# A language-model layer on one core: which engine copies the first probabilities, adds the word and position rows, and writes the first keys

## The reference

```python
h = gamma * norm(word_emb[ids] + pos_emb + type_emb[types]) + beta
a = norm(h)
k, q, v = heads(a @ Wk), heads(a @ Wq), heads(a @ Wv)          # 16 heads of 16
k, q = norm(k) * kln_w + kln_b, norm(q) * qln_w + qln_b        # over the 16 of a head
attn = softmax(where(causal, q @ k.T / 4, -inf))
h = h + (attn @ v) @ Wo + bo
x = norm(h)
scores = softmax(x @ gate_w.T); sel = top_k(scores + expert_bias, 2)
h = h + sum over the two chosen experts e of  score_e-weighted  (silu(xe @ w1[e]) * (xe @ w3[e])) @ w2[e]
```

## Time and profile before

| what | value |
|---|---|
| median of 3 runs | 545.32 us (545.27 to 545.44) |
| time of the profiled execution | 545.62 us |
| its span (first to last instruction) | 543.8 us |
| busy: PE, DVE, ACT, POOL | 501.2, 291.9, 250.7, 286.2 us |
| shares of the last-ending chain: PE, DVE, POOL, ACT | 79%, 5%, 5%, 4% |
| stretch 100 to 120 us, busy: PE, DVE, ACT, POOL | 18.52, 17.63, 17.50, 14.93 us of 20 |
| stretch 180 to 200 us, busy: PE, DVE, ACT, POOL | 17.16, 18.00, 16.35, 14.71 us of 20 |

### The profile page before, as it was taken

The page is one execution under the profiler, slowest core; times in us unless marked ns, Lnnn a source line. Parts: engine busy times, 40 slices in busy tenths (PEclk is TensorE's granted clock), DMA queues, the critical chain, the costliest instruction groups (busy, mean ns, idle before and its releaser), DMA issues.

```text
span 543.8 us, 13452 instructions
## 1 busy us (share of the span) xinstructions
PE 501.2 (92%) x4470; PEld 428.7 (79%) x4471; DVE 291.9 (54%) x759; ACT 250.7 (46%) x575; POOL 286.2 (53%) x532
## 2 busy tenths in 40 slices
PE   5877989998999888999999999999999999999991
PEld 2345666777776665499999999999999999999980
DVE  2778888889989887733333333333333333333330
ACT  1166788978997883243223322332233323332320
POOL 4678787677764675214543454345434454344432
PEclk9999999999999999999999999999999999999996
DMA  5007721101028672302212221122112221222221
GB/s 174 10 22 243 231 85 31 58 29 29 29 80 278 212 251 84 90 22 41 29 30 39 39 39 22 37 39 39 23 36 39 39 28 31 39 38 30 30 39 19
DMA packets 29962, 36.75 MB, mean 68 GB/s; under 512 B 8272, under 2 KB 23504, under 8 KB 29936
## 3 DMA queue, kind: packets, MB, share of 16 engines
q0 software_dynamic: 8352, 12.76, 13.8%
q1 hardware_dynamic: 20768, 22.61, 13.1%
q10 hardware_dynamic: 816, 1.06, 0.6%
HBM read 26.81 MB, written 9.50 MB: 67 GB/s over the span
## 4 chain that ended last, share of the span: by engine, by line
PE 79%; DVE 5%; POOL 5%; ACT 4%; issue 3%; DMA 2%; POOLq 0%; DVEq 0%; ACTq 0%
PE PS L1445 35%; PE PS L1456 18%; PE PS L1172 10%; PE PS L1296 5%; PE PS L1254 2%; PE PS L1395 2%; PE PS L1271 2%; DMA x_pair<-word_dram,idx 1%; PE PS L1180 1%; ACT work L628 1%; PE PS L1310 1%; PE PS L1243 1%; DVE nmax L879 1%; DMA out_dram<-x_pair,dst_c 1%; POOL arena L477 1%
## 5 line engine op out<-in xcount | busy, mean ns | idle before, releaser
L1445 PEld LDWEIGHTS PS<-work,arena 128*128 128x128 f32 x1716 | 197.6, 192 | 2.3 <-ACT work L744 0.4
L1445 PE MATMUL PS<-work,arena 128*128 128x128 f32 x1716 | 198.0, 275 | 0.0
L750 ACT ACTIVATE work<-PS 128x768 f32<-128x768 f32 x39 | 31.6, 810 | 197.2 <-PE PS L1445 197.2
L1456 PE MATMUL PS<-w_sb,work 128*128 x468 | 107.6, 379 | 0.7 <-DVE x_pair L1147 0.7
L1139 DVE TENSOR_TENSOR work<-work,PS 128x640 f32<-128x640 f32 x39 | 32.0, 821 | 138.0 <-ACT work L750 138.0
L1456 PEld LDWEIGHTS PS<-w_sb,work 128*128 128x128 f32 x468 | 85.9, 190 | 11.2 <-issue 1.1
L572 POOL DMA_INDIRECT out_dram<-x_pair,dst_c x39 | 79.2, 2030 | 21.9 <-POOL dst_c L571 20.5
L571 POOL COPY dst_c<-dest_i 128x1 int32 (+1 forms) x39 | 7.1, 183 | 138.7 <-DVE x_pair L1147 136.5
L628 ACT ACTIVATE work<-PS,nmax 128x128 f32<-128x128 f32 x256 | 72.0, 401 | 3.7 <-DVE nmax L879 3.7
L740 ACT ACTIVATE arena<-w_sb 128x1408 f32 x40 | 55.1, 1379 | 12.0 <-DVE er_i L1115 9.0
L1172 PE MATMUL PS<-ident,work 128*128 128x128 f32 x336 | 54.8, 276 | 1.8 <-ACT work L628 1.8
(11 more groups left out here) (172 smaller groups left out, 618.8 us busy)
## 6 DMA issues: line engine op xcount, KB each, us to landing
w_sb<-w_dram SPq DMA_DIRECT2D x16, 640.0 KB, 5.6
w_sb<-w_dram SPq DMA_DIRECT2D x8, 704.0 KB, 4.5
x_rows<-x SPq DMA_DIRECT2D x16, 128.0 KB, 2.3
out_dram<-arena SPq DMA_DIRECT2D x16, 128.0 KB, 2.4
w_sb<-w_dram SPq DMA_DIRECT2D x16, 64.0 KB, 6.2
w_sb<-w_qkv_dram ACTq DMA_DIRECT2D x1, 768.0 KB, 8.2
work<-x_rows,src_c POOLq DMA_INDIRECT x41, 2.8
out_dram<-x_pair,dst_c POOLq DMA_INDIRECT x39
```

What stands on the lines that cost most here:

```text
L1445: last = n.matmul(up_ps[p][:, i, c, :], ws[p][:, k, at:at + P], xT_sb[p][:, k, :], start=(k == 0), stop=(k == DK - 1))
L1456: last = n.matmul(PS[:, 7, 0:D], hT_sb[p][:, i, :], w2_sb[:, bass.ds(e, 1), i, :], start=(i == 0), stop=(i == FK - 1))
```

## The change

Five edits, all in the attention part:

1. From step 2 on, DVE makes the copy of group 0 of the turned probabilities (`transposed_first`, after `keys_out` in its queue). ACT keeps it in steps 0 and 1. The copy has its own semaphore, `probsT0_ready`; PE's `outputs` and `mask_banks` wait for both.
2. The addition of word rows and `x_base` moves from DVE to POOL (`x_sum`) for sequences 5 to 15, that is in steps 1 to 11. It stands after POOL's square roots at the start of the step and before the next `gather`.
3. From step 2 on, DVE's `sum_rows` (now only mean and variance) stands behind the normalization of sequence t-2 (`x2`), not ahead of it.
4. For sequences 0, 1 and 2 ACT writes the keys itself, ahead of the queries, and waits for `qk_ps` (PE's transposes) instead of `k_ready`; DVE's `keys_out` for these goes.
5. In step 0 ACT's `queries_out(1)` stands ahead of `transposed(2)`.

```diff
+        KEYS_BY_ACT = 3
...
+                def x_sum(u, q, n):
+                    pool.wait_ge(x_base_ready, u + 1)
+                    pool.wait_ge(gathered[q], 16 * (n + 1))
+                    g.tensor_tensor(x_in[q], x_in[q], x_base, ALU.add).then_inc(x_summed, 1)
...
+                    if valid(t + 4) and not at_step(t, 0):
+                        x_sum(t + 4, p, half(4))
                     if valid(t + 5):
                         gather(t + 5, 1 - p, link)
...
-                    a.activation(probsT[:, r * 512:(r + 1) * 512], PS[...], ACT.Copy).then_inc(probsT_ready, 1)
+                    a.activation(probsT[:, r * 512:(r + 1) * 512], PS[...],
+                                 ACT.Copy).then_inc(probsT0_ready if r == 0 else probsT_ready, 1)
...
                 def queries_out(u):
-                    act.wait_ge(k_ready, u + 1)
+                    if isinstance(u, int) and u < KEYS_BY_ACT:
+                        act.wait_ge(qk_ps, u + 1)
+                    else:
+                        act.wait_ge(k_ready, u + 1)
...
+                    if isinstance(u, int) and u < KEYS_BY_ACT:
+                        a.activation(kT.rearrange("p b s -> p (b s)"), PS[:, T_BANK, D:2 * D], ACT.Identity,
+                                     scale=cols_sb[:, 4:5], bias=cols_sb[:, 5:6]).then_inc(k_ready, 1)
...
                     transposed(0)
                     transposed(1)
+                    queries_out(1)
                     transposed(2)
-                    queries_out(1)
...
-                if valid(t):
+                if at_step(t, 1):
                     transposed(0)
...
+                def transposed_first():
+                    dve.wait_ge(probsT_ps, RG * t + 1)
+                    wait(dve, pv_done, t)
+                    v.tensor_copy(probsT[:, 0:512], PS[:, 0, :]).then_inc(probsT0_ready, 1)
...
+                    if isinstance(u, int) and u < EARLY:
+                        dve.wait_ge(x_base_ready, u + 1)
+                        dve.wait_ge(gathered[q], 16 * (n + 1))
+                        v.tensor_tensor(x, x, x_base, ALU.add).then_inc(x_summed, 1)
...
-                    keys_out(0)
...
+                if valid(t) and not at_step(t, 0) and not at_step(t, 1):
+                    transposed_first()
...
-                    keys_out(1)
...
-                    keys_out(2)
...
-                if valid(t + 4) and valid(t):
+                if valid(t + 4) and valid(t) and (at_step(t, 0) or at_step(t, 1)):
                     sum_rows(t + 4, p, half(4))
...
                     normalize(x2[p][:, :], row(u), 2).then_inc(x2_ready, 1)
+                if valid(t + 4) and valid(t) and not at_step(t, 0) and not at_step(t, 1):
+                    sum_rows(t + 4, p, half(4))
...
-                    pe.wait_ge(probsT_ready, RG * u + RG)
+                    pe.wait_ge(probsT0_ready, u + 1)
+                    pe.wait_ge(probsT_ready, (RG - 1) * u + RG - 1)
```

More of the change, by code:

```diff
@@ L224, in build_tower @@
         s_done, max_done, exp_done = sem("s_done"), sem("max_done"), sem("exp_done")
-        probsT_ps, probsT_ready, pv_done, o_ready = (
-            sem("probsT_ps"), sem("probsT_ready"), sem("pv_done"), sem("o_ready"))
+        probsT_ps, probsT_ready, probsT0_ready, pv_done, o_ready = (
+            sem("probsT_ps"), sem("probsT_ready"), sem("probsT0_ready"), sem("pv_done"), sem("o_ready"))
         o_raw_ready, o_back, oT_ps, oT_ready, wo_done = (
@@ L634, in transposed @@
                     wait(act, pv_done, t)
-                    a.activation(probsT[:, r * 512:(r + 1) * 512], PS[:, T_BANK if r == RG - 1 else r, :], ACT.Copy).then_inc(probsT_ready, 1)
+                    a.activation(probsT[:, r * 512:(r + 1) * 512], PS[:, T_BANK if r == RG - 1 else r, :],
+                                 ACT.Copy).then_inc(probsT0_ready if r == 0 else probsT_ready, 1)
                 def x2_out(u):
@@ L920, in sum_rows @@
                                                ALU.add).then_inc(x_base_ready, 1)
-                    dve.wait_ge(x_base_ready, u + 1)
-                    dve.wait_ge(gathered[q], 16 * (n + 1))
-                    v.tensor_tensor(x, x, x_base, ALU.add).then_inc(x_summed, 1)
+                    if isinstance(u, int) and u < EARLY:
+                        dve.wait_ge(x_base_ready, u + 1)
+                        dve.wait_ge(gathered[q], 16 * (n + 1))
+                        v.tensor_tensor(x, x, x_base, ALU.add).then_inc(x_summed, 1)
                     dve.wait_ge(x_summed, u + 1)
@@ L1235, in mask_banks @@
                     pe.wait_ge(exp_done, RG * u)
-                    pe.wait_ge(probsT_ready, RG * u - 1)
+                    pe.wait_ge(probsT0_ready, u)
+                    pe.wait_ge(probsT_ready, (RG - 1) * u - 1)
                     n.matmul(PS[:, RG - 2, 0:E], identb[:, :], mask[:, 0:E], start=True, stop=True)
@@ L1346, in step @@
                     if not edge or t > 0:
-                        pe.wait_ge(probsT_ready, RG * t)
+                        pe.wait_ge(probsT_ready, (RG - 1) * t)
                     transposes(qkn, 2 * DK, T_BANK).then_inc(qk_ps, 1)
```

## The result

The changed kernel takes 547.24 us (median of 6 runs, 546.82 to 549.05), the kernel before, timed in turn with it, 545.47 us (6 runs, 545.27 to 546.01). The ratio is 1.0038, with a 95% interval of 1.0027 to 1.0049: slower by 1.8 us. Forecast were 547.1 us and a range of 544.3 to 548.6.

The account below looks back on a forecast made before the run. No engine had much to give; PE's chain ran nearly unbroken in the loop, DVE, POOL and ACT bounding start and steps 12 to 15. Terms -2.1 +1.2 +0.7 +0.7 +0.6 +0.55 +0.1 = +1.75 us: median 547.1, range 544.3 to 548.6.

Parts of the forecast that it names:

- Start, -2.1: Before step 0: with early keys on idle ACT, PE's first scores start at about 29.1 instead of 31.24, -2.1 us.
- Step 1, +1.2: Step 1: POOL's sum stands behind its square root L437, giving back 1.2 of the 2.1 us gained.
- Steps 2 and 3, +0.7: Steps 2 and 3: POOL's sum and constant tables delay DVE's division and PE's transposes, +0.7 us.
- Steps 4 to 10, +0.7: Loop: longer wait order before PE's weight load, 0.16 us a pass, 0.64 in all, and a little for step 4.
- The ring: From step 2: POOL's sum, DVE's division and POOL's next square roots form a closed cycle of 10.93 us against 10.88.
- PE absorbs waits and ring: Rival, chance 0.23: the loop's wait list costs nothing, POOL's cycle stays just under the step; 546.0 us.
- Step 12, +0.6: Step 12: the copy moves DVE's division, making PE's transposes wait, +0.6 us.
- Step 14, +0.55: Step 14: DVE has no gap up to the maxima of step 15, so the copy costs +0.55 us.
- The copy, 0.60: DVE from step 2 on: group 0's copy takes 0.60 us, with ends 0.42 and 0.68.
- ACT's wait in front of L678: Sign, loop: if ACT's idle time before its copy does not grow, the prediction is wrong about the bound.
- ACT was the bound: Rival, chance 0.17: loop waits for ACT's exponentials are real, so fewer copies free -2.9 us; 544.2 us.
- The sum and `x2` block each other: Rival, chance 0.12: lock or register waits add 0.3 us to POOL's cycle from step 3 on; 549.1 us.

Follow-up runs that it names:

- e1: The kernel before with only the early keys on ACT and the changed order in step 0: 544.97 us, ratio 0.9994.
- e11: The e5 kernel with three more 128x512 matmuls on PE in step 0, behind the seven already there: 544.18 us, ratio 0.9969.
- e13: The e11 kernel with a dead 128x1 copy on DVE in step 1, behind two long-met waits: 543.49 us, ratio 0.9962.
- e2: The kernel before with only the sum moved to POOL and DVE's statistics behind x2: 547.74 us, ratio 1.0036.
- e4: The kernel before with only the copies' count split into two semaphores, all work where it was: 545.63 us, ratio 0.9992.
- e8: The changed kernel with one more small unread copy on POOL ahead of its sum in each loop step: 547.86 us, ratio 1.0036.
- e3: The kernel before with only the group 0 copy on DVE from step 2 on, with the two semaphores: 548.51 us, ratio 1.0047.
- e7: The changed kernel with ACT making the group 0 copy again from step 12 on: 545.95 us, ratio 1.0004.
- e10: The changed kernel with DVE's statistics of the sum ahead of x2 again in every step: 552.6 us, ratio 1.0127.
- e6: The changed kernel with DVE still adding the rows of sequence 5 in step 1: 546.21 us, ratio 1.0014.
- e5: The e1 kernel with six 128x512 matmuls in PE's idle time of step 1: 543.94 us, ratio 0.9968.
- e12: The e11 kernel with ACT's queries of sequence 1 behind its third copy in step 0 again: 544.12 us, ratio 0.997.

## Why the prediction was right

The direction, the start, step 1, step 3 and the price of the copy in step 12 came out as forecast. That the sum came out to 0.02 us (+1.75 forecast, +1.77 measured) is luck. Read from the table, with -2.1 for start and step 0, the terms were put too high by 1.29 us: 0.58 in steps 4 to 11, 0.25 in step 14, 0.17 in steps 2 and 3, 0.11 in step 12, 0.1 for the wait lists, 0.08 in step 1. Missing were 1.28 us: 0.56 in step 13 and 0.72 in and behind step 15.

- **Start, -2.1: right.** The first scores stand at 28.39 to 28.91 us in the ten kernels with early keys, at 30.75 to 31.24 in the four without: -2.3 between the means (28.67, 30.99), of which step 0 gives back 0.2 to 0.3 (the whole change, e1, e11, e13): about -2.1 is left.
- **Step 1, +1.2: right**, +1.12 in the change and +1.06 in e2. PE's transposes stand at 50.49 instead of 51.1, because this execution began early.
- **Steps 2 and 3, +0.7: right**, +0.53 and +0.57.
- **Steps 4 to 10, +0.7: the step that failed.** +0.16 in step 4, nothing behind it. "From the end of ACT's copy to PE's weight load it is ... 0.23": the longer wait came as forecast and cost nothing; in e4 a hidden gap of about 0.1 us in PE's rows took it. The ring was priced at 10.93 us against a step of 10.88. The step is 10.85 in the mean (79.10 to 144.22 for six steps), and e8 puts the ring 0.03 under it. So its size was off by about 0.1 us, and with it the sign. Of the rival "PE absorbs waits and ring" that half is true.
- **Step 12, +0.6: right**, +0.49. Step 13, which I expected free, has +0.56: 0.46 of it goes with the idle time in DVE's queue, which belongs to none of the edits and is gone in e13.
- **Step 14, +0.55: too much there, too little behind it.** +0.30, and +0.72 more in and behind step 15, where e3 has +0.87 and e7 +0.13. I had given step 15 room in DVE's queue; the copy stands there too, in front of the last routing work. With the copy left on ACT there (e7) this goes.
- **The copy, 0.60; the wait lists, +0.1.** 0.60 is what the next instruction stands behind it (103.12 to 103.72). The lists cost 0 (e4).

Of its own signs, two did not come. In step 12 PE waits 0.21 us for `o_n`, not 0.5. And ACT's wait in front of L678 has not grown: 11.1 us in eight steps before and after, 1.59 for 1.62 us in the rows above. The prediction called that a sign of being wrong about the bound; it was a bad sign. The time of the copy went elsewhere in ACT's step, 0.2 to 0.3 us of it into the wait for the keys, and PE's loop stayed as long as it was (-0.04).

Of the rivals, the runs speak against *ACT was the bound*: with a copy less, PE waits 2.0 us for the exponentials instead of 2.1. No run took work from ACT in the loop without giving it to DVE, so that is as far as it goes. *The sum and `x2` block each other* is right in its mechanism and wrong in its price. I had judged `x2` unblocked by a row of 0.41 us from step 3; in the first steps of a pass the same trace has 0.60 or 0.61, each ending 0.08 or 0.09 us behind POOL's `gather` (116.71 and 116.62 in the rows of e10). In the changed kernel it takes 0.66 to 0.81 us in the six steps in which it starts 0.06 to 0.22 us behind the sum, 0.48 or 0.49 where it starts 0.39 us behind, and 0.38 to 0.44 in seven of ten steps of e10. The Trainium skill, "SBUF — State Buffer" (section "SBUF: two separate sides"), calls the port pair of VectorE and GpSimd an exclusive lock held for the whole instruction; the trace agrees: `x2` ends 0.15 or 0.16 us behind the sum in all ten steps (104.42 and 104.26 in the rows above), whenever it starts. But it costs next to nothing, because the statistics behind it wait for the same sum and start at 104.34, 0.08 us behind it (0.03 or 0.04 where no `x2` is in the way). Put ahead of `x2`, they cost 0.45 us a step (e10): edit 3 is what made the sum bearable.

## What to carry to other kernels

Two engines' work moved in opposite directions can be free together and dear apart: undo each part by itself before you judge one. An idle engine is slack only if what it waits for does not come from itself; follow the wait round once, and load it by a known bit to measure the rest. A gain at the start of a pipeline stays only where the narrow engine (here POOL) gets it too, and where nothing is added in front of it: the early keys alone have a median 0.9 us lower here, within the noise, 1.6 to 1.8 with PE kept busy and 2.2 in the best version (e13, 543.49 us), and the other two moves spent all of it.

## What the runs showed of the hardware

- After an idle time of 1.26 to 1.45 us in step 1 PE's clock fell to 0.50 in the traces of e1, e4, e6, e7 and e8, and stayed at 1.00 in those of before, after, e2, e3 and e10, which have that idle time as well. It went with 0.75 and 0.86 us more in e4 and e1. With six matmuls in the gap of step 1 (e5, e11, e12, e13) it fell in none of four traces.
- In step 0 it fell in e5 and e7 at 35 us, with 1.5 us more there, half of it given back in step 1. In e2 and e3 it fell at 31 us, behind an idle time of 2.09 and 2.08 us and during the first scores (0.50 from 32 to 34 us), and step 0 was only 0.15 and 0.20 us longer; before and e4 have that idle time and kept 1.00. In e10 it fell in step 3, behind 2.02 us.
- A VectorE normalization of 128x256 (`x2`, one tensor input, 0.41 us alone) is held up by GpSimd's addition of two tiles (0.66 to 0.81 us, ending 0.15 us behind it) and by GpSimd's `gather` if it starts 0.50 to 0.60 us behind that one's start (0.59 to 0.69 us, ending 0.08 to 0.10 behind it; before, e1, e10, e13). Starting up to 0.49 us behind it, it took 0.38 to 0.46.
- One dead VectorE instruction and two waits took an idle time of 0.30 us without a releaser out of the queue 127 us later, and 0.45 us out of that step (e13). The cause stays open.
- A wait that is longer by 0.15 us can vanish in a gap for which the profile marks no idle time; only the distance of two starts shows it (0.57 against 0.44 us).
